# Attention with an FP8-style linear layer: a new slot plan, the product with V in one step, seven probability buffers

## The reference

```
xn  = (x - mean(x)) / sqrt(var(x) + 1e-5)
Q, K, V = xn @ W_q.T, xn @ W_k.T, xn @ W_v.T        # 16 heads of 16 each
Q, K = rope(Q), rope(K)
p   = softmax(causal(Q K^T / 4))                     # 512 x 512 per head
att = (p V as 512 x 256) @ W_o.T
ffn = fake_quant_fp8(xn) @ fake_quant_fp8(weight).T + bias   # one scale over all of xn, one over weight
out = x + att + ffn
```

## Time and profile before

| | us |
|---|---|
| median of 3 runs (440.33 to 442.19) | 440.36 |
| the profiled execution | 439.77 |
| span of its trace | 438.0 |
| busy: PE, PEld | 384.9, 205.9 |
| busy: DVE, ACT, POOL | 355.3, 290.6, 245.4 |
| first scores, slot 0, end of slot 159 | 32.3, 60.37, 425.25 |

### The profile page before, as it was taken

The page is one execution under the profiler, slowest core; times in us unless marked ns, Lnnn a source line. Parts: engine busy times, 40 slices in busy tenths (PEclk is TensorE's granted clock), DMA queues, the critical chain, the costliest instruction groups (busy, mean ns, idle before and its releaser), DMA issues.

```text
span 438.0 us, 9484 instructions
## 1 busy us (share of the span) xinstructions
PE 384.9 (88%) x2990; PEld 205.9 (47%) x2990; DVE 355.3 (81%) x1380; ACT 290.6 (66%) x487; POOL 245.4 (56%) x266
## 2 busy tenths in 40 slices
PE   7998987878879988998899898989899998898886
PEld 7685543333434544454445444545445433353335
DVE  3899679999888988898888979887989797879104
ACT  3529538567765777587866776676677677669751
POOL 5444263365559548556666666676666565245750
...
GB/s 280 307 146 71 1 94 79 73 2 97 123 0 75 52 157 62 75 27 94 148 75 1 98 171 61 15 52 216 15 62 49 183 38 74 2 99 4 49 49 49
DMA packets 27810, 36.40 MB, mean 83 GB/s; under 512 B 3984, under 2 KB 25872, under 8 KB 26320
## 3 DMA queue, kind: packets, MB, share of 16 engines
...
...
## 4 chain that ended last, share of the span: by engine, by line
PE 63%; ACT 16%; DVE 10%; issue 7%; POOL 2%; DMA 1%; ACTq 0%; POOLq 0%; SPq 0%; DVEq 0%
PE o_ps L1047 15%; ACT prob L803 12%; PE st_ps L943 9%; PE m_ps L927 9%; PE m_ps L1005 7%; PE m_ps L982 7%; PE s_ps L962 5%; DVE scratch L657 4%; PE m_ps L989 2%; PE s_ps L899 2%; DVE prod L605 2%; DMA q_st<-shift 1%; PE m_ps L1013 1%; DVE prod L604 1%; DVE amax L593 1%
## 5 line engine op out<-in xcount | busy, mean ns | idle before, releaser
L803 ACT ACTIVATE prob<-st_ps,exp_scale 128x512 f32<-128x512 f32 x320 | 202.9, 689 | 98.9 <-PE st_ps L943 98.2
L657 DVE CUSTOM_DVE_ANT_0 scratch<-s_ps,causal 128x512 bf16<-128x512 f32 (+3 forms) x512 | 221.3, 484 | 35.8 <-PE s_ps L962 33.8
L510 POOL TENSOR_SCALAR_AFFINE_SELECT prob<-prob 128x512 f32<-128x512 f32 (+1 forms) x160 | 90.1, 565 | 147.4 <-ACT prob L803 147.3
L943 PE MATMUL st_ps<-q_st,k_st 50*128 50x128 f16 (+3 forms) x512 | 108.9, 303 | 35.4 <-ACT prob L803 26.9
L962 PE MATMUL s_ps<-k_st,q_st 48*128 48x512 f16 (+3 forms) x512 | 109.7, 306 | 4.7 <-DVE rowmax L657 4.4
L943 PEld LDWEIGHTS st_ps<-q_st,k_st 50*128 50x128 f16 x512 | 35.2, 94 | 121.1 <-ACT prob L803 74.6
L1047 PE MATMUL o_ps<-prob,v_sb 128*17 128x512 f32 (+3 forms) x1024 | 82.8, 441 | 1.7 <-POOL prob L510 0.9
L962 PEld LDWEIGHTS s_ps<-k_st,q_st 48*128 48x128 f16 x512 | 34.5, 95 | 15.9 <-DVE rowmax L657 9.0
L657 DVE DVE_READ_ACCUMULATOR2_ANT rowmax<- 128x1 f32 x512 | 41.1, 80 | 0.0
L1047 PEld LDWEIGHTS o_ps<-prob,v_sb 128*17 128x17 f32 x1024 | 23.2, 97 | 30.0 <-issue 23.0
L982 PE MATMUL m_ps<-wv_sb,xnT 128*128 128x256 f32 x128 | 33.7, 408 | 1.5 <-ACT v_sb L810 1.3
...
## 6 DMA issues: line engine op xcount, KB each, us to landing
...
```

The source lines that it names most:

```text
L510: eng.affine_select(out=ap, in_=ap, compare_op=ALU.is_ge, fill=0.0, base=0, pattern=pat, channel_multiplier=-1).then_inc(masked, 1)
L657: eng.tensor_tensor_reduce(scratch[:, at % 3, col:col + w], s_ps[at % 3][:, col:col + w], causal[:, T - w:T], 1.0, NEG, ALU.add, ALU.max, ...
L803: eng.activation(prob[u][:, half * T:(half + 1) * T], st_ps[ST_BANK[2 * s + half]][:, :], ACT.Exp, scale=exp_scale[:, 0:1]).then_inc(exp_d ...
L943: mm = eng.matmul(st_ps[ST_BANK[i]][:, col:col + T - kb * P], k_rows(n, h, ROWS + SHIFT, slice(kb * P, (kb + 1) * P)), q_rows(n, h, ROWS + ...
```

## The change

- `OFFSETS` gets new slots for all shared steps. By slot of a batch they now stand: fin in 19, 0, 2, 5; o in 3, 4, 7, 8; at in 9 and 13; qk in 10, 12, 15, 17; v in 14 and 18 (of the batch before); mt in 16, 1, 6, 11. Before, `fin` was in 11, 14, 16, 18, `o` in 3 to 6, `at` in 8, 9, 12, 14, `qk` in 8, 10, 13, 15, `v` in 0 and 2, `mt` in 16, 1, 7, 12. `fin` of batch n comes about eight slots later, and that of batch 6 in slots of its own.
- `pv` of a group is one step in slot 5g+6, except for the last group. With seven probability buffers in turn, `exp` of slot 5j+7 waits for the product of slot 5j+6.
- Two buffers where there was one: V, prod, rot, the residual, the quantized input, and the turned attention output for four row blocks. `at` turns two row blocks in one step, and ACT copies both with one instruction.
- The chain through DRAM, the quantization and the copies get new slots; `high_x` moves from slot 5 to 6, `split_x` from 6 to 8; the copy of V moves ahead of other ACT work.
- Startup: mean and variance of batches 4 and 5 move from DVE to ACT (16 activations with an accumulator: Identity, then Square); a slot -11 is added, in which the first two `qk` of batch 1 stand (before: slots -7 and -6); `v` of batch 0 moves to slots -2 and -1; `largest(0)` moves to slot 0; after the wait on `low_done` PE does 24 idle matmuls in place of 26 and a wait on a DMA.

```diff
+PROBS = 7
...
-OFFSETS = {("v", 0): 0, ("mt", 1): 1, ("v", 1): 2, ("o", 0): 23, ("o", 1): 24, ("o", 2): 25, ("o", 3): 26, ("mt", 2): 7,
-           ("at", 0): 28, ("qk", 0): -32, ("at", 1): 29, ("qk", 1): -30, ("fin", 0): 31, ("at", 2): 32, ("mt", 3): 12,
-           ("qk", 2): -27, ("fin", 1): 34, ("at", 3): 34, ("qk", 3): -25, ("fin", 2): 36, ("mt", 0): -4, ("fin", 3): 38}
+OFFSETS = {("v", 0): -6, ("v", 1): -2, ("mt", 0): -4, ("mt", 1): 1, ("mt", 2): 6, ("mt", 3): 11,
+           ("o", 0): 23, ("o", 1): 24, ("o", 2): 27, ("o", 3): 28, ("at", 0): 29, ("at", 1): 33,
+           ("fin", 0): 39, ("fin", 1): 40, ("fin", 2): 42, ("fin", 3): 45,
+           ("qk", 0): -30, ("qk", 1): -28, ("qk", 2): -25, ("qk", 3): -23}
+LAST_FINS = {("fin", 0): 30, ("fin", 1): 32, ("fin", 2): 34, ("fin", 3): 35}
 SPREAD = [(17, "spread", 0, 0), (19, "spread", 0, 1)]
-EARLY = {("qk", 0): -7, ("qk", 1): -6, ("qk", 2): -5, ("qk", 3): -4}
-CHAIN = {("rotate", 0): -29, ("high", 0): -28, ("low", 0): -26, ("write", 0): -25, ("rotate", 1): -24, ("high", 1): -23,
-         ("low", 1): -21, ("write", 1): -20, ("read", 0, 0): -19, ("read", 0, 1): -16, ("read", 1, 0): -12,
-         ("read", 1, 1): -11}
-EARLY_CHAIN = {("rotate", 0): -5, ("high", 0): -5, ("low", 0): -4, ("write", 0): -3, ("rotate", 1): -2, ("high", 1): -2,
-               ("low", 1): -1, ("write", 1): 0, ("read", 0, 0): -1, ("read", 0, 1): 3, ("read", 1, 0): 9,
-               ("read", 1, 1): 10}
-TURN_SLOT = {2: -LEAD, 3: -LEAD + 1, 4: -LEAD + 2, 5: -LEAD + 3, 6: -LEAD + 5, 7: -LEAD + 7}
+EARLY = {("qk", 1, 0): -LEAD - 1, ("qk", 1, 1): -LEAD - 1, ("qk", 1, 2): -9, ("qk", 1, 3): -8, ("v", 0, 0): -2, ("v", 0, 1): -1}
+CHAIN = {("rotate", 0): -27, ("high", 0): -24, ("low", 0): -23, ("write", 0): -21, ("rotate", 1): -21, ("high", 1): -19,
+         ("low", 1): -18, ("write", 1): -16, ("read", 0, 0): -19, ("read", 0, 1): -15, ("read", 1, 0): -12,
+         ("read", 1, 1): -7}
+EARLY_CHAIN = {("rotate", 0): -10, ("high", 0): -9, ("low", 0): -8, ("write", 0): -7, ("rotate", 1): -7, ("high", 1): -6,
+               ("low", 1): -5, ("write", 1): -4, ("read", 0, 0): -5, ("read", 0, 1): -1, ("read", 1, 0): 4,
+               ("read", 1, 1): 5}
+TURN_SLOT = {2: -10, 3: -8, 4: -7, 5: -6, 6: -4, 7: -3}
...
+DVE_STATS, ACT_STATS = (0, 1, 2, 3, 6, 7), (4, 5)
...
-    items = [(EARLY[kind, k] if (kind, n) == ("qk", 1) else SLOTS * n + off, order[kind, k], kind, n, k)
...
-FIRST_SLOT, END_SLOT = -LEAD, SLOTS * NB + 3
+FIRST_SLOT, END_SLOT = -LEAD - 1, SLOTS * NB + 3
...
-    first, last, loop = (24, 25, 26, 27, 28), (6, 7, 11, 12, 14), (16, 17, 21, 22, 24)
+    first, last, loop = (24, 25, 26, 27, 29), (8, 9, 12, 13, 15), (11, 13, 14, 24, 26)
...
-        v_sb = sb("v_sb", [P, NQ, H, VW])
-        prob = [sb(f"prob{u}", [P, PAIR]) for u in range(5)]
+        v_sb = sb("v_sb", [P, 2, NQ, H, VW])
+        prob = [sb(f"prob{u}", [P, PAIR]) for u in range(PROBS)]
         heads = sb("heads", [P, NG, T])
-        prod = sb("prod", [P, 4, T])
-        rot = sb("rot", [P, 2, T])
+        prod = sb("prod", [P, 2, 4, T])
+        rot = sb("rot", [P, 2, 2, T])
...
-        attnT = sb("attnT", [P, 2, NC, P])
-        x_res = sb("x_res", [P, NQ, D])
-        xq = sb("xq", [P, NC, T], BF16)
-        stats = sb("stats", [P, 2, NQ, 6])
-        mv_b = sb("mv_b", [P, 2, NQ, 2])
-        ve = sb("ve", [P, 2, NQ])
-        nmean = sb("nmean", [P, 2, NQ])
+        attnT = sb("attnT", [P, NQ, NC, P])
+        x_res = sb("x_res", [P, 2, NQ, D])
+        xq = sb("xq", [P, 2, NC, T], BF16)
...
+        def prob_of(n, s):
+            return prob[(SLOTS * n + s) % PROBS]
...
-            if n > 0:
-                eng.wait_ge(low_done[1 - w], 2 * (n + w))
-            if (n, w) == (1, 0):
-                eng.wait_ge(low_done[0], 2)
-            dst = rotated_in(n, w)
-            eng.tensor_tensor(dst[:, 0, :], prod[:, 0, :], prod[:, 2, :], ALU.subtract).then_inc(rotated[w], 1)
-            eng.tensor_tensor(dst[:, 1, :], prod[:, 1, :], prod[:, 3, :], ALU.add).then_inc(rotated[w], 1)
+            wait_past(eng, low_done[w], 2 * n)
+            eng.tensor_tensor(rot[:, w, 0], prod[:, w, 0], prod[:, w, 2], ALU.subtract).then_inc(rotated[w], 1)
+            eng.tensor_tensor(rot[:, w, 1], prod[:, w, 1], prod[:, w, 3], ALU.add).then_inc(rotated[w], 1)
...
-                for g, off in enumerate((-3, 2, 8, 13)):
+                for g, off in enumerate((-3, 2, 7, 12)):
...
-                n = batch_at(slot, 39)
-                if n is not None and n < NB - 1:
-                    store(n)
+                for n in range(NB - 1):
+                    if slot == SLOTS * n + (47 if n < NB - 2 else 37):
+                        store(n)
...
+            def mean_of_sum(i):
+                eng.wait_ge(ln_sum, NQ * (i + 1))
+                eng.tensor_scalar(nmean[:, ACT_STATS[i], :], sums[:, i, :], -1.0 / D, None, ALU.mult).then_inc(ln_mean, 1)
...
-                n = batch_at(slot, -34, 2)
+                n = batch_at(slot, -32, 2)
...
-                n = residual_at(slot, 29, 17)
+                n = residual_at(slot, 31, 17)
...
-            largest(0)
             statistics(2, 3)
-            statistics(4, 5)
...
+                if slot in range(0, 2 * NB, 2):
+                    largest(slot // 2)
+                weight_step(slot)
...
+            def add_up(i):
+                eng.wait_ge(x_in[ACT_STATS[i]], 16)
+                wait_past(eng, ln_sum, NQ * i)
+                for t in range(NQ):
+                    eng.activation(unread[:, t, :], x_of(ACT_STATS[i])[:, t, :], ACT.Identity, accum_out=sums[:, i, t:t + 1])\
+                       .then_inc(ln_sum, 1)
+            def add_squares(i):
+                eng.wait_ge(ln_mean, i + 1)
+                eng.wait_ge(ln_sum, NQ * len(ACT_STATS))
+                wait_past(eng, ln_square, NQ * i)
+                for t in range(NQ):
+                    eng.activation(unread[:, t, :], x_of(ACT_STATS[i])[:, t, :], ACT.Square,
+                                   bias=nmean[:, ACT_STATS[i], t:t + 1], accum_out=squares[:, i, t:t + 1])\
+                       .then_inc(ln_square, 1)
...
-                g, u = divmod(s, 5)
-                if n > 0 or g > 0:
-                    eng.wait_ge(pv_done, 8 * n + 2 * (g - 1) + (1, 1, 2, 2, 2)[u])
+                wait_past(eng, pv_done, (SLOTS * n + s - PROBS) // 5 + 1)
...
+            def copy_at(n, i, bank):
+                eng.wait_ge(full["at"], 2 * n + i + 1)
+                wait_past(eng, full["fin"], 4 * (n - 1) + 2 * i + 2)
+                eng.copy(attnT[:, 2 * i:2 * i + 2], bank[:, :].rearrange("p (q c n) -> p q c n", q=2, c=NC))\
                    .then_inc(at_copied, 1)
...
+            add_up(0)
             high(0, 0)
             copy_turned(1)
+            add_up(1)
             high(0, 1)
             high_x(1)
+            add_squares(0)
+            add_squares(1)
...
-                n = batch_at(slot, -35, 2)
+                n = batch_at(slot, -34, 2)
...
+            def turn_two(n, i, bank):
+                turn_attn(n, 2 * i, bank, 0)
+                return turn_attn(n, 2 * i + 1, bank, D)
...
-            def first_block(n, g):
-                pv(n, g, 2, ((0, (0, 1)),)).then_inc(pv_done, 1)
-            def other_blocks(n, g):
-                pv(n, g, 5, ((1, (2, 3)), (3, (2, 3)), (2, (4,)))).then_inc(pv_done, 1)
...
-            keep_busy(16)
-            eng.wait_ge(parts_out[1], 16)
-            keep_busy(10)
+            keep_busy(24)
...
+                if slot == SLOTS * NB - 2:
+                    pv(NB - 1, NG - 1, 2, ((0, (0, 1)),))
                 if slot == SLOTS * NB:
                     pv(NB - 1, NG - 1, 4, ((1, (2, 3)), (3, (2, 3))))
                 n = batch_at(slot, 21)
                 if n == NB - 1:
                     pv(n, NG - 1, 5, ((2, (4,)),)).then_inc(pv_done, 1)
-                elif n is not None:
-                    other_blocks(n, NG - 1)
                 for g in range(NG):
-                    n = batch_at(slot, 5 * g + 3)
-                    if n is not None:
-                        first_block(n, g)
                     n = batch_at(slot, 5 * g + 6)
-                    if n is not None and g < NG - 1:
-                        other_blocks(n, g)
+                    if n is not None and (n, g) != (NB - 1, NG - 1):
+                        pv(n, g, 5, ((0, (0, 1)), (1, (2, 3)), (3, (2, 3)), (2, (4,)))).then_inc(pv_done, 1)
```

More of the change, by code:

```diff
@@ L539, in _ @@
                     mask(*at)
+                if slot == -LEAD - 1:
+                    invert(4)
+                    invert(5)
                 if slot == -LEAD + 2:
@@ L546, in _ @@
                         step(eng, n, w)
-                if slot == 22:
+                if slot == 23:
                     eng.wait_ge(wquant, 8)
@@ L668, in norm @@
                 if qb == 0:
-                    wait_past(eng, full["at"], 4 * n)
+                    wait_past(eng, full["at"], 2 * n)
```

(24 more changed lines are left out.)

150 lines of the change are left out of this document (75 added, 75 removed).

## The result

The changed kernel takes 462.73 us (median of 4 runs, 459.89 to 467.29), the kernel before 441.27 on the same chip: ratio 1.046 (95% interval 1.0415 to 1.0512). The profiled execution took 459.89 us, its span is 458.1 against 438.0.

The account below looks back on a forecast made before the run. It took the dealing of PE's work over slots as the bound. From 439.77 us: -5.9 startup, -3.8 batches 0 and 1, -4 x 2.7 steady batches, -2.05 batch 6, -2.6 batch 7: 414.6, 415 as median; range 405 to 427.

Parts of the forecast that it names:

- What bounds the kernel: Steady batches: no engine is full; the dealing of PE's work over slots leaves PE still about 6.2 of 46.26 us.
- PE's need by slot: Steady batch under the new dealing: PE needs from 1.13 us (o, at) to 3.05 (V-product, mt) a slot, 39.7 a batch.
- The walk: Both lists followed from slot 3: 43.5 us a steady batch, gain 2.7; bounds 41.5 and 46.2.
- The merged product: V-product of a group in one step for two: saves 0.4 us a batch, bounds 0 and 0.98; waits cost nothing.
- Batches 0 and 1: First two batches, bound by DVE: 93.5 us at DVE 94% busy, for 97.3; -3.8, bounds 0 and -6.
- Batch 7: Last batch: two V-steps leave, three more fin come; 38.8 us for 41.43, the end behind slot 159 untouched.
- Startup: First score to slot 0: 22.2 us for 28.07, two ropes moved ahead; -5.9, bounds -8 and 0.
- The table load: ACT's function table: Square, new in the startup, needs no switch, 0 us; bound 2.6 us.
- (c): Rival, slower: ropes waiting for their own slot's product block DVE's queue; 50.2 us a batch, about 453 us; chance 0.05.
- (b): Rival: stalls only change place, steady batches stay at 46.2 us, only the ends gain; about 428 us; chance 0.16.
- (a): Rival: banks carry more than allowed, DVE becomes the bound at 41.5 us a batch; about 404 us; chance 0.14.
- (d): Rival: dealing does nothing, something unseen (DMA, queue) sets 46.2 us, startup gives its gain back; 440 us; chance 0.03.

Follow-up runs that it names:

- e2: Changed kernel with ACT's first copy of the heads' output one slot later, in slot 8 behind that slot's exps: 447.64 us, kernel before 444.74.
- e4: Kernel before with the merged V-product in slot 5g+6 and seven probability buffers, all else as before: 469.38 us, kernel before 444.74.
- e3: Changed kernel with the V-product of a group in two steps again, slots 5g+3 and 5g+6: 438.14 us, kernel before 444.74.
- e11: Changed kernel with heads copy in slot 8, batch 6's residual three slots earlier, two-step V-product, unread filler matmuls, 12 idle pairs: 421.09 us, kernel before 442.26.

## Why the prediction was wrong

It said 415 us, and the range of 405 to 427 missed by 36. By its own steps:

- **What bounds the kernel.** The dealing, with PE, ACT and DVE running dry in turns: right. The change without the merged product and the late steps, and with fillers, is worth 17 us, 12 of them in the steady batches.
- **PE's need by slot.** Right at full clock: the group slot 3.02 us for 3.05, the merged product 2.28 for 2.30. The durations were all read from rows at a granted clock of 1.00, and the sum used them for every batch. **That is the step that failed.** The clock column of the earlier trace rows shows 0.80, 0.90 and 0.97 up to slot 0 and in batches 0 and 1, and it was never priced: nothing in the sum, the bounds or the rivals asked what PE is granted in and behind "six light slots", a phrase of the walk itself. The runs show 95 us at 1.2 GHz for 24 before, in batches 0, 1 and 7 and in slots 9 to 11 of the steady ones.
- **The miss in four parts.** From the 415 forecast to 462.73 it is 47.7 us. In the order of the table, fillers and the shorter idle stretch take away 15.5, the late steps 16.1, the two-step product 8.5, and 7.7 are left.
- **The walk, 43.5 us a steady batch.** Slots 10 to 12 forecast 7.8, 13 and 14 4.5, 15 to 2 18.2; e2 measured 8.08, 4.49 and 18.66, and 12.38 for slots 3 to 9 where 13.0 was forecast. Sum 43.6, so the 43.5 came true once the copy was moved, with misses of up to 0.6 that cancel. In the changed kernel slots 3 to 9 took 14.37, since the walk gave the copies of the heads no wait ("chain steps, copies" at nothing); that wait costs 0.6 us a batch at full clock and 1.5 to 2.8 more through the clock. For a moved step it asked whether its own inputs are there. It did not ask who waits for it: `o` moved past a copy that writes what it reads.
- **The merged product.** Forecast -0.4 a batch, at nothing else; at full clock it is +0.5 in the new plan (43.6 for 43.1 in two steps) and +1.5 in the old (e4), and more through the clock. In the new plan ACT waits 10.8 us a batch for scores with the merged product (e2) and 9.0 with two steps (e3). The fixed 0.10 us is real. That the first step had filled light slots (1.13 us without it in 3, 8 and 13, by the prediction's own list) was never charged.
- **Batches 0 and 1**, forecast 93.5: 110.3. In e11, at full clock and with the product in two steps, they are 96.7. The rest of the miss, 3.2, is there too; the DVE share of 94% that was assumed came out at 90 (87.49 of 96.68). No row stood behind the 94: in the earlier trace rows it is 90 as well (87.94 of 97.28).
- **Batch 6**, forecast 39.5: 43.5, and 40.4 in e2. **Batch 7**: 38.8, and "The end behind slot 159 is untouched". Batch 7 with the end should have been some 51.6; it was 58.8, and 53.7 when mended. "Stores and residuals have a second buffer" was true and beside the point: POOL's step was listed one slot behind its reader.
- **Startup**, forecast slot 0 at 54.5: 60.06. 24 idle matmuls (x48 in the row) in place of 16, a wait and 10 ran at once, until 30.98 (instructions of PE in order of time, changed kernel):

```profile
25.59 5.62 PE L922 MATMUL s_ps<-ident 128*128 128x128 f32 x48 [0.68 <-DVE parts L350]
...
30.98 3.00 PE L950 MATMUL m_ps<-x_parts,wq_parts 128*128 128x512 f32 x12
...
33.91 0.39 PE L985 MATMUL s_ps<-k_st,q_st 48*128 48x512 f16 x1
```

  The prediction allowed 32.8 for the first score, it came at 33.91. The stage behind it took 26.15 us, for 22.2, part of it at half clock. With 12 pairs and fillers (e11) the score is at 31.63 and slot 0 at 56.17. That leaves 24.54 for a forecast of 22.2: the gain was over-rated by 2.3 as well.
- **The table load** at 0: right. The list of groups still has one (last line of the first rows), and so has that of every run here. Square came with no switch, so the price that the Trainium skill gives for one ("ScalarE: Activation LUTs", What ACT_TABLE_LOAD costs) was not met in any run.
- **The rivals.** (c), the one on the slower side, did not happen, though the kernel is slower: DVE waits for Q/K products 1.9 us in the whole of batch 3, the bound was 4, and slots 15 to 2 came out as forecast. The 0.05 was on the wrong mechanism. (b) would have looked right by the steady batches (46.2 forecast, 45.7 to 47.0 measured), but e2 excludes it: the batch is 43.6 with one copy moved. (a), 41.5 a batch, fails since no version here has a steady batch under 43.0; (d), that something unseen sets 46.2, since e2 has 43.6.

With all of it mended (e11) the plan gives 421: against the forecast 1.7 more up to slot 0, 3.2 in batches 0 and 1, 1.0 in batch 6 and 2.1 behind it, and 1.7 less in the four steady batches.

What stays open: how much of the 24 us at 1.2 GHz in each of batches 0 and 1 would go if `v` of batch 0 stood in slots 0 and 2 again, with no filler; the old startup order with the new dealing; and a second `heads` buffer in place of the later copy. None of these was tried. Nor is it shown why the same program gets 95 us of half clock in one execution and 109 in another.
